# A fused MoE and adapter kernel: three matmuls of the last stage on 64-row halves of the array

## The reference, cut to what matters

```python
x = x + _L0_ffn_ref(_L0_cond_ref(x, cond, W0), ...)        # 64 experts, top 8, capacity 256
x = x + _L1_ffn_ref(_L1_cond_ref(x, W, A, Bm, scal, ad), base_w, base_b, router_w, router_b, lora_A, lora_B)

def _L1_cond_ref(x, W, A, Bm, scalings, adapter_idx):      # x (32, 128, 1024), one adapter per batch entry
    H = einsum('btd,od->bto', x, W)
    xa = einsum('btd,brd->btr', x, A[adapter_idx])         # rank 16
    delta = einsum('btr,bor->bto', xa, Bm[adapter_idx]) * scalings[adapter_idx]
    return H + delta

def _L1_ffn_ref(x, ...):                                   # 8 experts, top 2, rank 16
    result = x @ base_w.T + base_b
    gate = top-2 softmax weights of (x @ router_w.T + router_b)
    return result + 2.0 * sum_e gate[e] * (x @ lora_A[e]) @ lora_B[e]
```

## Time and profile before

| | us |
|---|---|
| median of 3 runs | 2403.81 |
| lowest and highest of them | 2399.71, 2403.90 |
| the profiled execution | 2391.3 |
| its span in the trace | 2389.5 |
| granted TensorE clock over the span, as a share of 2.4 GHz | 0.996 |

### The profile page before, as it was taken

One profiled execution on the slowest core, in us unless ns is written; L12 is line 12 of the kernel. 1 busy time (PEld: TensorE's weight loads), 2 busy tenths in 40 slices (PEclk: granted clock), 3 DMA queues, 4 the chain that ended last, 5 costly groups with the idle time before them and its releaser, 6 DMA issues.

```text
span 2389.5 us, 35288 instructions
## 1 busy us (share of the span) xinstructions
PE 2355.3 (99%) x12762; PEld 2075.4 (87%) x12762; DVE 1734.9 (73%) x2874; ACT 1371.2 (57%) x2256; POOL 1409.5 (59%) x1032
## 2 busy tenths in 40 slices
PE   7988999999999999999999999999999999999999
PEld 5677888888888888888888888888889999999999
DVE  6887888888878878888888888887852255555554
ACT  5766777777767767777777776777751211111110
POOL 4028777787778777777777777777710132222221
PEclk9999999999999999999999999999999999999999
DMA  9998999899998998989989899899875354444441
GB/s 337 382 334 281 280 289 279 277 284 288 283 284 286 284 284 277 285 273 289 280 276 286 280 284 284 273 286 285 275 189 119 87 140 130 130 130 130 130 121 56
DMA packets 250352, 582.33 MB, mean 244 GB/s; under 512 B 82745, under 2 KB 106682, under 8 KB 250178
## 3 DMA queue, kind: packets, MB, share of 16 engines
q1 hardware_dynamic: 183202, 401.18, 51.2%
q0 software_dynamic: 55584, 160.02, 25.8%
q10 hardware_dynamic: 11392, 18.88, 2.1%
HBM read 456.51 MB, written 123.45 MB: 243 GB/s over the span
## 4 chain that ended last, share of the span: by engine, by line
PE 94%; DVE 1%; DMA 1%; POOL 1%; ACT 1%; issue 1%; ACTq 0%; SPq 0%; DVEq 0%; POOLq 0%
PE ps L789 26%; PE ps L802 22%; PE ps L898 16%; PE ps L788 13%; PE ps L856 5%; PE ps L785 4%; PE ps L658 2%; PE ps L891 2%; PE ps L786 2%; PE ps L668 1%; PE ps L871 1%; POOL Xg L567 1%; PE ps L681 0%; PE ps L680 0%; DMA bmR<-accd 0%
## 5 line engine op out<-in xcount | busy, mean ns | idle before, releaser
L789 PE MATMUL ps<-XX,HR 128*128 128x512 f32 x2688 | 961.6, 397 | 0.0
L788 PE MATMUL ps<-XX,LR 128*128 128x256 f32 x2688 | 751.5, 280 | 0.0
L567 POOL DMA_INDIRECT Xg<-yd,idx x504 | 654.0, 1298 | 158.5 <-issue 153.2
L1486 DVE TENSOR_TENSOR LR<-raw,HR 128x1536 fp32r<-128x1536 f32 x384 | 657.1, 1752 | 3.1 <-ACT HR L1053 3.1
L789 PEld LDWEIGHTS ps<-XX,HR 128*128 128x128 f32 x2688 | 506.2, 188 | 104.5
L1053 ACT ACTIVATE HR<-raw 128x1536 fp32r<-128x1536 f32 x384 | 556.6, 1479 | 11.9 <-DMA raw<-in_L_ffn_wd 10.3
L788 PEld LDWEIGHTS ps<-XX,LR 128*128 128x128 f32 x2688 | 508.5, 189 | 18.2 <-DVE LR L1486 0.6
L589 POOL DMA_INDIRECT accd<-ot,toki x128 | 255.9, 2000 | 159.5 <-ACT ot L1107 139.4
L898 PE MATMUL ps<-MH,xT 128*128 128x392 f32 x1536 | 335.9, 344 | 0.0
L802 PE MATMUL ps<-LR,hH 128*128 128x512 f32 x768 | 302.5, 394 | 0.0
L802 PE MATMUL ps<-HR,hL 128*128 128x512 f32 x768 | 301.1, 392 | 0.0
(11 more groups left out here) (214 smaller groups left out, 3299.6 us busy)
## 6 DMA issues: line engine op xcount, KB each, us to landing
raw<-in_L_ffn_wd SPq DMA_DIRECT2D x128, 768.0 KB, 4.9
raw<-in_L_ffn_wg SPq DMA_DIRECT2D x126, 768.0 KB, 7.5
raw<-in_L_ffn_wu SPq DMA_DIRECT2D x126, 768.0 KB, 7.0
yd<-yrow ACTq DMA_DIRECT2D x32, 512.0 KB, 6.7
x<-accd SPq DMA_DIRECT2D x32, 512.0 KB, 5.2
out<-osb SPq DMA_DIRECT2D x31, 512.0 KB, 3.0
xt<-in_x SPq DMA_DIRECT2D x25, 512.0 KB, 8.0
accd<-xt SPq DMA_DIRECT2D x25, 512.0 KB, 6.4
```

Of the source, the lines that this page charges most:

```text
L567: eng.indirect_dma_start(Xg[:, c, q, :], None, yd4, bass.IndirectOffsetOnAxis(ap=idx4[:, e % 4, i:i + 1], axis=0))\
L788: eng.matmul(bank(out, 0, CAP), wl, xx[:, 0:CAP], start=False, stop=False)
L789: mm = eng.matmul(bank(out), wh, xx, start=False, stop=(k == 7))
L1486: eng.tensor_tensor(LR[:, (n + 2) % NHL, :], raw[:, n % NRAW, :], HR[:, (n + 2) % NHL, :].bitcast(F32), ALU.subtract).then_inc(s_L, 1)
```

## The change

The operands of `adapter` stand twice, in rows 0 to 47 and in rows 64 to 111. Column groups 0 and 2 take rows 0 to 63 of `xaS` and `m8`, column group 1 takes rows 64 to 127. Each is a matmul on a tile of 64 rows by 128 columns, at row 0 or at row 64, in place of one with 128 rows. In the program as built nothing changes its place on any engine.

For that, `copy_3` writes six copies (96 columns) in place of three, `low_a` is two instructions of 16 rows in place of one, `gather_m` fetches 112 rows in place of 48 (520 KB for 223 KB: 1160 columns of 4 bytes each), and the list `midx` is worked out at the start with three more DVE instructions. Rows 48 to 63 of the fetched block hold copies of a real row, and meet zeros in `xaS`.

```diff
-        pq = sb("pq", [P, 4], F32, rt)
+        pq = sb("pq", [P, 6], F32, rt)
@@ gather_m (POOL)
-                eng.indirect_dma_start(m8[0:3 * R, t % 2, :].bitcast(F32), None, m8d,
-                                       bass.IndirectOffsetOnAxis(ap=midx[0:3 * R, t:t + 1], axis=0))\
+                eng.indirect_dma_start(m8[0:P - R, t % 2, :].bitcast(F32), None, m8d,
+                                       bass.IndirectOffsetOnAxis(ap=midx[0:P - R, t:t + 1], axis=0))\
                    .then_inc(d_gm[t % 2], 16)
@@ adapter (PE)
                     i = o if g == 2 else 0
-                    mm = eng.matmul(bank(b0 + g, i, i + z - a), xaS[:, :], m8[:, t % 2, a:z], start=False, stop=True,
+                    h = slice(64, 128) if g == 1 else slice(0, 64)
+                    mm = eng.matmul(bank(b0 + g, i, i + z - a), xaS[h, :], m8[h, t % 2, a:z], start=False, stop=True,
                                     skip_group_check=True)
@@ vector, at the start
-            eng.tensor_scalar(pq[:, 0:1], pf[:, 0:1], float(R), float(P - R), ALU.is_ge, ALU.mult)
-            ch.link(eng.tensor_scalar(pq[:, 1:2], pf[:, 0:1], float(2 * R), float(P - R), ALU.is_ge, ALU.mult))
+            ch.link(eng.tensor_scalar(pq[:, 4:5], pf[:, 0:1], float(P // 2), float(-P // 2), ALU.is_ge, ALU.mult))
+            ch.link(eng.tensor_tensor(pq[:, 5:6], pq[:, 4:5], pf[:, 0:1], ALU.add))
+            eng.tensor_scalar(pq[:, 0:1], pq[:, 5:6], float(R), float(P - R), ALU.is_ge, ALU.mult)
+            ch.link(eng.tensor_scalar(pq[:, 1:2], pq[:, 5:6], float(2 * R), float(P - R), ALU.is_ge, ALU.mult))
             ch.link(eng.tensor_tensor(pq[:, 2:3], pq[:, 0:1], pq[:, 1:2], ALU.add))
-            ch.link(eng.tensor_tensor(pq[:, 3:4], pq[:, 2:3], pf[:, 0:1], ALU.add))
+            ch.link(eng.tensor_tensor(pq[:, 3:4], pq[:, 2:3], pq[:, 5:6], ALU.add))
+            ch.link(eng.tensor_scalar(pq[:, 3:4], pq[:, 3:4], float(2 * P + R - 1), None, ALU.min))
@@ copy_3 (DVE)
-                eng.tensor_copy(xas[:, 0:3 * R].rearrange("p (h r) -> p h r", h=3),
-                                bank(b2, o, o + R).unsqueeze(1).to_broadcast([P, 3, R])).then_inc(s_xa, 1)
+                eng.tensor_copy(xas[:, :].rearrange("p (u h r) -> p u h r", u=2, h=4)[:, :, 0:3, :],
+                                bank(b2, o, o + R).unsqueeze(1).unsqueeze(1).to_broadcast([P, 2, 3, R])).then_inc(s_xa, 1)
@@ low_a (DVE)
-                eng.tensor_tensor(xaS[2 * R:3 * R, :], ps[2 * R:3 * R, 6, 0:P], xaS[2 * R:3 * R, :].bitcast(F32),
-                                  ALU.subtract).then_inc(s_xal, 1)
+                for a in (2 * R, 2 * R + P // 2):
+                    mm = eng.tensor_tensor(xaS[a:a + R, :], ps[a:a + R, 6, 0:P], xaS[a:a + R, :].bitcast(F32),
+                                           ALU.subtract)
+                mm.then_inc(s_xal, 1)
```

## The result

The changed kernel takes 2410.05 us (median of 8 runs), the kernel before 2403.10 us (8 runs): ratio 1.0035, 95% interval 1.0025 to 1.0045, so 8.4 us slower (6.0 to 10.8). (The medians themselves stand 6.95 us apart. The ratios and intervals in this document are the recorded ones, and they aren't quotients of the two medians.) The profiled execution has a span of 2411.2 us against 2389.5. That is 21.7 us more, and not all of it is the change's: 10.2 us of it lie ahead of the first expert, where both kernels have the same work but for three small DVE instructions.

What follows compares the result with a forecast made beforehand. PE, busy in 99% of the span, was taken as the bound. 31 tiles at +0.27 us (8.4) and 0.8 for the last gave +9.2 us: 2403.8 + 9.2 = 2413.0 us, range 2398 to 2418.

Steps and rivals of the forecast that it cites:

- The way in: On PE, main to adapter: load starts 0.27 us after the last main matmul, exposed for 0.11; +0.20 us.
- The way out: On PE, adapter back to main: load starts 0.28 us after group 2, exposed for 0.11; +0.21 us.
- The overlap: Adapter groups 0 and 1 on different rows work at the same time: 0.14 us saved, 0.18 if loads overlap too.
- A tile: Tiles 0 to 30, one adapter call each: net +0.27 us, between 0.23 and 0.41; 31 calls make 8.4 us.
- The last tile: Two adapter calls with other work between, so two switches and no overlap: 2 x 0.41 = 0.8 us.
- The fetch: gather_m with 112 rows takes about 0.1 us more on POOL, data wanted some 29 us later: hidden, no cost.
- The tight place at the gate: POOL's addition holds DVE's L1741; mg has 0.09 us of room; a later POOL lets L1741 go first: no cost.
- Rival 4: DVE or POOL late, so PE waits for mg: 3 us per 0.1 us, from a fetch of about 1.5 us; chance 0.02.
- Rivals 1 to 3: Free switch, 5.5 us off, 0.17; cheap switch, no change, 0.11; switch costs and nothing overlaps, 13.5 us slower, 0.10.
- the free and the cheap switch: Adapter's row switch costs nothing, 5.5 us off, 0.17; or costs 0.15 a tile, within 1 us of before, 0.11.
- no overlap: Adapter's switch costs and its fp32r matmuls on different rows don't overlap: 13.5 us slower; chance 0.10.

Runs made afterwards that it cites:

- quad32: Kernel before with the adapter's three matmuls on 32-row tiles at rows 0, 32 and 64, low part of xa left out; ratio 1.0010, tile 15.052 us.
- half_only: Kernel before with the three adapter matmuls contracting rows 0 to 63 instead of 0 to 127, nothing else changed; ratio 1.0058, tile 15.397 us.
- three_switch: Kernel before with adapter matmuls on rows 0 to 63 and called apart, three switches a tile; 2425.37 us (one run), tile 16.163 us.
- same_half: Changed kernel with column group 1 on rows 0 to 63 as well; ratio 1.0055 to the kernel before, tile 15.397 us.
- wide_fetch: Kernel before with only the fetch of m8 widened from 48 to 112 rows, with its index list; ratio 1.0014, tile 15.037 us.
- full_rows: Changed kernel with its three adapter matmuls back on all 128 rows; 2392.98 us (one run), tile 15.029 us.
- the two tuned kernels: Kernel before and changed kernel, both with tile 1's m8 fetch later and the last bias addition waiting for mg of tile 29; ratios 0.9985 and 1.0017.

## Why the prediction was right, by its steps

- **The way in**: 0.27 us until the load starts and 0.11 for the load. Both as forecast (2101.78 to 2102.05; in quad32 and half_only the same).
- **The way out**: forecast 0.28 until the load starts. Half_only's trace gives 0.26 by the distances of single starts, so the switch costs 0.39, not 0.41. Confirmed by half_only (0.390) and three_switch (0.385 each). L717, which I read as showing the same as L818, has 64 columns to stream where L818 has 8: worked out from L717 the wait is 0.13 - 0.03 + 0.16 = 0.26, an estimate that fits better.
- **The overlap**: this term was mis-sized. I let the three loads follow each other at 0.11 us and credited 0.14 us. The loads for different rows run together, as in the row with both at 2102.05, and a whole matmul is saved: 0.173 by same_half. The bound of 0.18 was the right value. L725's own loads hinted at it, four of about 0.10 us each in 0.16 us, though in bf16 and with half the clock:

```profile
150.37 0.16 PEld L725 LDWEIGHTS ps<-c0s,oh 32*128 32x128 bf16 x4 [1.18 <-issue]
```

- **A tile**: 0.216 us more in place of 0.27, just under the bound of 0.23, since both small errors point the same way. In 31 calls that is 1.7 us too much. By the starts in the list, from the last `main` matmul to the next one behind the adapter is 0.81 us, where I had named 0.98 as the sign: behind an exposed load the list starts a matmul together with its load, so 0.11 is to be added, and 0.92 is 0.21 more than the 0.71 of before.
- **The last tile**: by the distances of starts its two switches cost 0.388 us each, 0.78 in all, forecast 0.8. The 1.07 us from tile 30 on hold these, two calls at 0.216, and 0.16 less of PE's wait for `mg` in tile 30. Between the two tuned kernels, where that wait is gone, the same stretch differs by 1.24.
- **The fetch**: here a step failed, though not so that the result changed sign. I wrote that its data are wanted 29 us later and that DMA is under half busy, from a stretch in the middle of the stage. At its start two fetches go out together, and the DMA engines are full: their busy share (the list goes over 1) is 1.06 to 1.14 from 1908 to 1920 us before the change, against 0.45 in the earlier trace rows, and 1.06 to 1.11 in the same 12 us after it. Before the change PE already waited 0.2 us there for a load of x. It was a wait with no room left, and wide_fetch shows that the wider fetch lengthens it to 1.8 us. I had looked at who needs the fetched data, not at who shares the queue.
- **The tight place at the gate**: the forecast that PE doesn't wait there is right, but not for my reason. I expected L1741 to get ahead of POOL and be free. POOL's fetch grew by 0.05 us, not 0.1; DVE's operation is listed 0.03 us ahead of POOL's and was held all the same, for 2.46 us. And what I called 0.09 us of room was half that, as a semaphore's way is in it. With 128 rows PE does wait (wide_fetch, 0.03 us a tile, and full_rows, 0.02). What saved the changed kernel is the switch itself, 0.2 us that PE spends between the adapter and the gate's transpose; `mg` ends some 0.25 us ahead of its load there. Rival 4's point of decision, a fetch of 1.5 us, was wrong by far: without the switch 0.92 us is enough. The changed kernel's rows:

```profile
2103.85 2.45 DVE L1747 SCALAR_TENSOR_TENSOR g<-zr,e 128x8 f32<-128x8 f32 x1
2103.88 2.39 POOL L637 TENSOR_TENSOR x<-x,bias 128x1024 f32<-128x1024 f32 x1
...
2106.81 0.29 DVE L1753 TENSOR_TENSOR mg<-ps,gate 128x128 f32<-128x128 f32 x1
...
2107.36 0.14 PEld L880 LDWEIGHTS ps<-ident,mg 128*128 128x128 f32 x1
```

- **Rivals 1 to 3** are out: half_only against the free and the cheap switch, same_half against no overlap. What spoke for the cheap switch, L702's load 0.04 us behind the last columns, is the way of a semaphore. That load waits for `macc`, which DVE had finished 0.05 us before:

```profile
143.55 0.22 DVE L1362 SCALAR_TENSOR_TENSOR macc<-zr,macc 128x64 bf16<-128x64 f32 x1
```

So the mechanism and the size of the switch were right, but the sum of 9.2 us comes as near the 8.4 as it does in part by luck. PE's own terms are 31 x 0.216 + 0.78 = 7.5 us, 1.7 less than I had, and 1.9 us of wait in tile 1 were missed. The fall of the clock behind that wait, 1.5 us more in the profiled execution, came once in the six traces that have a wait of over 1 us in tile 1. How often it comes was not settled. The measurement, 6.0 to 10.8, can't tell 7.5 from 9.2.

The Trainium skill's rule in "TensorEngine Tiling (Array Packing)", section Tiling Modes, that a change of mode drains the engine, agrees with half_only, quad32 and three_switch. The same page of the Trainium skill lists 128x64 among the modes, and with that rows 8 don't agree: products with 64 and with 128 stationary columns alternate there at 0.12 us. The 4 ns between starts that the Trainium skill gives in "TensorE: Matmul & The Clock Gate", in its part on packing small matmuls, agree with the pair at 2102.05 too; what they don't count is the switch around the pair.

## What to carry to other kernels

Packing short contractions into parts of the array pays when a whole run of such matmuls stands together: count 0.39 us for each time the stream goes from full tiles to smaller ones and back, and 0.18 us for each matmul (of 392 columns) that disappears. By these numbers it takes three saved matmuls for each switch there and back. When a fetch is widened, look at the place where several of them start together and at what else waits for DMA there, not only at who needs its data. And where a step has under 0.1 us of room, take the semaphore's way, 0.05 us here, off before calling it room.

## What the runs showed of the hardware

- Going from 128-row matmuls to ones with 64 rows and back costs 0.385 to 0.390 us (three_switch, half_only): the first weight load comes 0.27 us after the start of the last full matmul, the load back 0.26 us after that of the last small one, and both are then exposed for 0.11. With 32 rows the first wait is the same 0.27 us, and the price is about 0.40 (quad32: 0.045 a tile and 0.35 saved).
- Weight loads for different rows of the array run at the same time, and so do fp32r matmuls behind them: two on 64 rows, three on 32 rows, within 0.01 us. The matmuls took no longer for it (0.44 us listed, as for a single one in three_switch).
- Going from 64 stationary columns to 128 costs nothing, though that too is a smaller tile. Behind products with 32 columns the 128-column load comes 0.13 us after the start of the last one, of which its own 64 streamed columns take 0.03. No run here changed the columns alone.
- A DVE operation with two inputs in SBUF on 8 columns is held through a whole addition of POOL (2.4 us), through two in a row (4.72 us), and even where it is listed 0.03 us ahead of POOL's, in one tile of quad32 0.13 us. With POOL elsewhere it takes 0.17 us (three_switch). That agrees with the shared port pair in the Trainium skill ("SBUF — State Buffer", SBUF: two separate sides), but for its rule that the one that starts first gets the pair, as far as listed starts can tell.
